# Two transformer layers with experts on one core: neighbours' steps at other places in the expert loops, unread matmuls in TensorE's waits, weight remainders in VectorE's waits

## The chip, the cores and the metric

The kernel runs on one NeuronCore of a Trainium2 chip. The metric is the device time of one launch in microseconds (us). Five engines take part: TensorE (PE in the rows, PEld for its weight loads), VectorE (DVE), ScalarE (ACT), GpSimd (POOL) and SyncE (SP), which issues all DMAs. Each engine runs its own list of instructions in order and waits on semaphores for the others.

## What is computed

Four sequences of 1024 tokens, 128 wide, go through two layers. Each is attention, add, layer norm, mixture of experts, add, layer norm:

```python
x = L0_attn_x                                        # (4, 1024, 128)
x = _layernorm(x + _L0_attn_ref(x, Wqkv, Wout))      # causal, 16 heads of 8, scores clipped
x = _layernorm(x + _L0_ffn_ref(x, Wg, W1, W2, W3))   # 8 experts, silu(x W1) * (x W2), W3, best 2
x = _layernorm(x + _L1_attn_ref(x, w_qkv, w_out, b)) # full attention, rotary, 16 heads
x = _layernorm(x + _L1_ffn_ref(x, rW1, ..., be2))    # 4 experts, gelu, best 2, router with a hidden layer
```

## The kernel before

There are five stages: the projections of the first layer, causal attention (to 300 us), the **first experts** (to 681 us), full attention (to some 1366 us) and the **last experts**. Every expert runs on all tokens; the gates make the choice.

**Expert stages.** The tokens are cut into eight chunks of 512. A chunk is 16 steps (`SPC`), a step is one slice of 128 hidden units. All products are made in three parts, from the upper halves and the remainders ("lo") of both factors. In step n of the first experts TensorE issues, in this order, what stands *beside* the step (`pe_beside`), the six matmuls of the hidden slice n+3 (`pe_hidden`, L1031) and the three of the product of slice n (`pe_product`, L1134). In the last experts the hidden slice has three matmuls and leads by five steps. VectorE does in its step n the multiply of slice n (L1447), the remainder of slice n-1 (L1436), what stands beside step n-2 (n-4 in the last experts, `LATE`), and in every second step the weighing of one expert's output by its gate (`dve_weigh`, L1427). ScalarE does silu (L1240) and the upper half (L1233) of a slice, and then what stands beside step n-2.

**Beside.** While chunk c runs, the chunk ahead ("front", c+1) is prepared and the chunk behind ("back", c-1) is finished. The steps of `plan` say at which n each piece stands: `o_proj` output projection, residual and statistics; `norm` the normalise of the front (L1292, tile xs); `x_turn` its transposes on TensorE (L946) and the two copies on ScalarE (L1209, L1210); `router` the gate scores (L1102) and the best two (from L1300); `weigh` gate weights; `g_turn` gates transposed; `y_turn` the transposes of the back's sum y_sb (L1053), residual and statistics (L1354); `norm2` its normalise (x_out) and a copy on ScalarE (L1190); `x2_turn`, `q`, `k`, `v` the next layer's projections (L1066, L1072). In the last experts `hidden` and `router` are the router's two layers (L1094, L1108). ScalarE's list has the copy of x_out ahead of the copies of `x_turn` where both stand beside the same step. `x2_turn` also waits for the front's best two (semaphore gate_pre), since it overwrites the bank with the gate scores.

**Ahead of the first experts** the front of chunk 0 is made with nothing running beside it. There VectorE also makes the remainders w_lo of the two hidden weights (L1486, after the normalise) and of the third weight, w3_lo (L1490, printed as w_lo too), after everything else.

**Behind the first experts** the back of chunk 7 is made with nothing beside it, apart from the first maxima of full attention: a "pair" is two score matmuls (L689) and one VectorE maximum over 1024 columns (L808), through a ring of two banks. Eight pairs stand beside the back (`BESIDE_BACK`), twenty more follow in `pe_full`, then the scores and the rounds of attention begin (16 rounds; in each, ScalarE makes 64 exponentials of 512 columns, L771).

## Time and profile before

| | us |
|---|---|
| median of 3 runs | 1602.66 (1599.79 to 1603.99) |
| the profiled execution | 1611.3 |
| its span in the trace | 1609.5 |
| TensorE busy | 1471.5 (91%) |
| VectorE busy | 1400.4 (87%) |
| ScalarE busy | 1202.9 (75%) |
| GpSimd busy | 307.5 (19%) |

No engine is idle long, and which one sets the pace changes from stage to stage. The page is therefore read by stage: the granted clock of TensorE first (full speed is 2.4 GHz, half is 1.2 GHz), then TensorE's idle times and what ended each.

### The profile page before, as it was taken

How to read it: one execution, taken by the hardware profiler on the slowest of the kernel's cores; microseconds unless marked ns; L12 is line 12 of the kernel's file. 1: busy time of each engine (PE TensorE's matmuls, PEld its weight loads, DVE VectorE, ACT ScalarE, POOL GpSimd, SP SyncE). 2: the span in 40 equal slices, each digit the busy share in tenths (PEclk: the TensorE clock that was granted, in tenths of full speed). 3: DMA queues.
4: the chain of work that ended last, by engine and by line, in shares of the span. 5: the costliest groups of instructions: out<-in, count | busy, mean ns of one | idle time of the engine just before them, and what ended most of it. 6: DMA issues, size and time to landing. Idle time of an engine off the chain costs nothing.

```text
span 1609.5 us, 32282 instructions
## 1 busy us (share of the span) xinstructions
PE 1471.5 (91%) x11200; PEld 797.1 (50%) x11200; DVE 1400.4 (87%) x2394; ACT 1202.9 (75%) x1897; POOL 307.5 (19%) x325
## 2 busy tenths in 40 slices
PE   7989898689999999969999999999999998999996
PEld 4333333377777777623333333333333334777775
DVE  5899999878888988887999999999999973788886
ACT  4999999644445454417999999999999986777775
POOL 0000000234455454420000000000000001234333
PEclk9899999799999998966999999999999997999999
DMA  6636432131224431111111111111111110211211
GB/s 203 203 106 182 120 102 86 49 107 40 96 93 127 128 108 66 66 41 51 46 37 37 46 45 38 42 37 36 37 36 36 37 32 28 69 56 63 75 56 40
DMA packets 71026, 116.76 MB, mean 73 GB/s; under 512 B 23808, under 2 KB 33920, under 8 KB 70272
## 3 DMA queue, kind: packets, MB, share of 16 engines
q1 hardware_dynamic: 70912, 115.21, 23.5%
q8 instruction: 75, 1.23, 0.3%
q14 instruction: 39, 0.32, 0.1%
HBM read 73.49 MB, written 41.16 MB: 71 GB/s over the span
## 4 chain that ended last, share of the span: by engine, by line
PE 61%; DVE 15%; ACT 10%; issue 10%; POOL 1%; DMA 1%; DVEq 0%; ACTq 0%; SPq 0%; POOLq 0%
PE full_o L718 14%; PE hid_pair L1031 12%; PE max_pair L689 11%; ACT cprobs L491 7%; PE bank L1134 7%; DVE negmax_h L808 5%; PE score L703 4%; PE causal_o L463 3%; PE triple L447 2%; PE bank L1066 2%; ACT o_sb L779 1%; DVE st L1284 1%; PE hid_pair L952 1%; PE bank L1094 1%; DVE hid_lo L1458 1%
## 5 line engine op out<-in xcount | busy, mean ns | idle before, releaser
L771 ACT ACTIVATE probs<-score 128x512 f32<-128x512 f32 x1024 | 546.6, 596 | 89.5 <-PE score L703 69.5
L808 DVE TENSOR_REDUCE negmax_h<-max_pair 128x2 f32<-128x1024 f32 x512 | 588.6, 1216 | 24.9 <-PE max_pair L689 24.8
L718 PE MATMUL full_o<-probs,v_st 128*32 128x256 f32 x4096 | 337.9, 403 | 17.7 <-ACT o_sb L779 17.7
L703 PE MATMUL score<-q_st,k_st 32*128 32x512 f32 x1024 | 319.9, 510 | 2.6 <-ACT probs L771 2.6
L689 PE MATMUL max_pair<-k_st,q_st 32*128 32x512 f32 x1024 | 264.7, 515 | 12.2 <-DVE negmax_h L808 10.8
L491 ACT ACTIVATE cprobs<-triple 128x1536 f32<-128x1536 f32 x192 | 258.4, 1713 | 5.2 <-PE triple L447 5.2
L689 PEld LDWEIGHTS max_pair<-k_st,q_st 32*128 32x128 f32 x1024 | 97.8, 188 | 236.7 <-DVE negmax_h L808 179.9
L1240 ACT ACTIVATE act_s<-hid_pair 128x512 f32<-128x512 f32 x128 | 76.7, 599 | 149.5 <-PE hid_pair L1031 149.5
L1031 PE MATMUL hid_pair<-x_hi,w_hi 128*128 128x512 f32 x384 | 171.3, 446 | 1.8 <-DVE x_lo L1401 1.0
L521 DVE TENSOR_SCALAR cprobs<-cprobs 128x1536 f32<-128x1536 f32 (+6 forms) x272 | 160.7, 618 | 2.9 <-ACT cprobs L491 2.9
L463 PE MATMUL causal_o<-cprobs,v_st 128*32 128x512 f32 (+3 forms) x1536 | 156.2, 502 | 2.2 <-DVE cprobs L521 2.2
L718 PEld LDWEIGHTS full_o<-probs,v_st 128*32 128x32 f32 x4096 | 83.3, 109 | 150.0 <-issue 94.5
L703 PEld LDWEIGHTS score<-q_st,k_st 32*128 32x128 f32 x1024 | 141.6, 187 | 28.8 <-ACT probs L771 19.5
L1031 PE MATMUL hid_pair<-x_lo,w_hi 128*128 128x512 f32 x384 | 154.6, 403 | 0.0
L1031 PE MATMUL hid_pair<-x_hi,w_lo 128*128 128x512 f32 x384 | 154.3, 402 | 0.0
L447 PE MATMUL triple<-q_st,k_st 32*128 32x512 f32 (+3 forms) x768 | 101.5, 429 | 28.7 <-ACT cprobs L491 26.0
L447 PEld LDWEIGHTS triple<-q_st,k_st 32*128 32x128 f32 x768 | 47.6, 186 | 135.5 <-ACT cprobs L491 127.1
L1248 ACT ACTIVATE hid_hi<-hid_pair,be 128x512 fp32r<-128x512 f32 x128 | 89.0, 695 | 24.9 <-PE hid_pair L1031 17.9
L1134 PE MATMUL bank<-hid_hi,w_hi 128*128 128x512 f32 x256 | 101.9, 398 | 1.4 <-DVE qk_lo L1436 1.3
L1134 PE MATMUL bank<-hid_hi,w_lo 128*128 128x512 f32 x256 | 101.4, 396 | 0.0
L568 POOL COPY v_st<-v_all 128x256 f32<-128x256 f32 x32 | 12.7, 400 | 434.6 <-PE causal_o L463 246.3
L520 DVE SCALAR_TENSOR_TENSOR cprobs<-cprobs,bound 128x256 f32<-128x256 f32 (+4 forms) x160 | 92.3, 577 | 3.9 <-ACT cprobs L491 2.5
(157 smaller groups left out, 2001.8 us busy)
## 6 DMA issues: line engine op xcount, KB each, us to landing
gate_all<-gate_scr SPq DMA_DIRECT2D x48, 512.0 KB, 4.3
o_scr<-o_sb SPq DMA_DIRECT2D x64, 256.0 KB, 2.1
k_st<-k_scr SPq DMA_DIRECT2D x64, 128.0 KB, 2.8
q_st<-q_scr SPq DMA_DIRECT2D x128, 64.0 KB, 2.5
k_st<-k_scr SPq DMA_DIRECT2D x64, 96.0 KB
q_st<-q_scr SPq DMA_DIRECT2D x64, 96.0 KB
q_scr<-qk_hi SPq DMA_DIRECT2D x18, 256.0 KB, 4.6
k_scr<-qk_hi SPq DMA_DIRECT2D x18, 256.0 KB, 4.5
```

The lines of the kernel that those rows point to most:

```text
L447: last = nc.tensor.matmul(triple[n % 2][:, bk, off:off + w], k_st[p][rows, kt * P:(kt + 1) * P], q_st[p][rows, q0:q0 + w], start=True, sto ...
L463: last = nc.tensor.matmul(causal_o[qc][SLOT * j:SLOT * (j + 1), c0:c0 + w], v_st[p][:, kt, j, :], cprobs[at % CP][:, bk, off:off + w], sta ...
L491: nc.scalar.activation(cprobs[n % CP][:, :, :], triple[n % 2][:, :, :], ACT.Exp, scale=SCALE).then_inc(L.exp_done, 1)
L520: nc.vector.scalar_tensor_tensor(edge, edge, float(np.exp(-CLIP)), limit, ALU.max, ALU.min)
L521: ins = nc.vector.tensor_scalar(plain, plain, float(np.exp(-CLIP)), float(np.exp(CLIP)), ALU.max, ALU.min)
L689: last = nc.tensor.matmul(ring[slot][:, k, :], q_st[p][rows, qt * P:(qt + 1) * P], k_st[p][rows, half * CH:(half + 1) * CH], start=True, s ...
L703: nc.tensor.matmul(sbank[L.score_bank(e)][:, :], k_st[p][rows, kt * P:(kt + 1) * P], q_st[p][rows, q0:q0 + w], start=True, stop=True, tile ...
L718: last = nc.tensor.matmul(full_o[SLOT * j:SLOT * (j + 1), cols], v_st[p][:, kt, j, :], probs[s % NP][:, j, cols], start=(kt == 0 and part ...
L771: nc.scalar.activation(probs[s % NP][:, L.HEADS[j], :], sbank[L.score_bank(e)][:, :], ACT.Exp, scale=SCALE).then_inc(L.exp_done, 1)
L808: nc.vector.tensor_reduce(negmax_h[:, qt // TPC, half, heads[0]:heads[1] + 1:2, qt % TPC], ring[slot][:, :, :], AXX, ALU.max, negate=True) ...
L1031: last = nc.tensor.matmul(hbank[2 * k + n % h_banks[layer]], w[:, slice_of(n)], x[:, :], start=(a == 0), stop=(a == 2))
L1134: last = nc.tensor.matmul(y_bank[e % 2], w, x, start=(f == 0 and a == 0), stop=(f == per - 1 and a == 2))
```

## The change

1. **Steps of the first experts' plan** are spread: y_turn 2 to 3, norm2 4 to 6, x2_turn 6 to 8, q 7 to 9, k 8 to 11, v 9 to 12, norm 3 to 4, x_turn 4 to 6, router 5 to 7, weigh 8 to 10, g_turn 10 to 13. The pairs beside the last back follow them. GpSimd's order gets the additions of y_sb (`pool_add`) moved between its other work.
2. **Steps of the last experts' plan** from x_turn on come one step later (x_turn, hidden, router, weigh); the gates are transposed in step 2 of their chunk (`GATES_AT`).
3. **Unread matmuls** (`pe_keep_busy`: ident times the rope table, fp32, 512 columns or half of it, into a bank that nobody reads then): one before the front of chunk 0, three after its step 1, one after its step 6; two and two in steps 2 and 3 of the last back; one of 256 columns after each of the twenty pairs.
4. **Remainders**: w_lo of the first weight goes before VectorE's wait for the output projection, that of the second behind the statistics, w3_lo behind the normalise and before x_lo.

```diff
-    BESIDE_BACK = {1: (0,), 2: (1,), 4: (2, 3), 7: (4,), 8: (5, 6), 9: (7,)}
+    BESIDE_BACK = {2: (0,), 3: (1,), 6: (2, 3), 9: (4,), 11: (5, 6), 12: (7,)}
...
             for m in first_pairs(L):
                 pe_pair(pe, L, 0, 0, m, m, m % 2)
+                pe_keep_busy(bank[0], 1, CH // 2)
...
-        for pl, steps in ((plan[0], (2, 4, 6, 7, 8, 9, 1, 1, 3, 4, None, 5, 8, 10)),
-                          (plan[1], (5, 7, None, None, None, None, 1, 1, 3, 6, 8, 11, 13, None))):
+        for pl, steps in ((plan[0], (3, 6, 8, 9, 11, 12, 1, 1, 4, 6, None, 7, 10, 13)),
+                          (plan[1], (5, 7, None, None, None, None, 1, 1, 3, 7, 9, 12, 14, None))):
...
-        GATES_AT, WEIGH_AT = 1, 1
+        GATES_AT, WEIGH_AT = 2, 1
...
+        BUSY_FRONT, BUSY_BACK = {1: 3, 6: 1}, {2: 2, 3: 2}
...
+        def pe_keep_busy(to, many, cols):
+
+            for _ in range(many):
+                nc.tensor.matmul(to[:, 0:cols], ident[:, :], rope_a[:, 0:cols], start=True, stop=True)
...
             if layer == 0:
+                pe.wait_ge(rope_loaded, 16 * 2)
+                pe_keep_busy(hbank[0], 1, CH)
                 for n in range(SPC):
                     pe_beside(pe, st, n, None, 0, 0, layer)
+                    if n in BUSY_FRONT:
+                        pe_keep_busy(hbank[0], BUSY_FRONT[n], CH)
...
                     pe_pair_beside_back(pe, layers[1], n)
+                    if n in BUSY_BACK:
+                        pe.wait_ge(st.v_saved, 2 * B - 1)
+                        pe_keep_busy(bank[2], BUSY_BACK[n], CH)
...
-                if n == (plan[0].norm, plan[1].x_turn)[layer]:
-
-                    for k in range(2):
+                if layer == 0 and n == plan[0].norm:
+                    dve.wait_ge(st.w3_upper, 1)
+                    nc.vector.tensor_tensor(w3_lo[:, :, :], w3[:, :, :], w3_hi[:, :, :].bitcast(F32),
+                                            ALU.subtract).then_inc(st.w3_lower, 1)
+                for k in ((0,) if n == plan[0].o_turn - 1 else (1,) if n == plan[0].o_proj else ()) if layer == 0 else (
+                        (0, 1) if n == plan[1].x_turn else ()):
```

**VectorE ahead of the first experts**, from the division (ot) on, before:

```order
L1377 TENSOR_TENSOR ot<-o_raw,o_rcp 128x512
L553 RECIPROCAL s_rcp<-s_raw 128x64
L1384 TENSOR_TENSOR res<-x_tm,bank 128x512
L1284 BN_STATS st<-res 128x6 x4
L1287 BN_AGGR mv<-st 128x2 x4
L1292 TENSOR_SCALAR xs<-res,mv,rstd 128x128 x4
L1486 TENSOR_TENSOR w_lo<-w_raw,w_hi 128x2048 x2
L1401 TENSOR_TENSOR x_lo<-xt,x_hi 128x512
```

The same stretch after, with the changed kernel's line numbers:

```order
L553 RECIPROCAL s_rcp<-s_raw 128x64
L1503 TENSOR_TENSOR w_lo<-w_raw,w_hi 128x2048
L1398 TENSOR_TENSOR res<-x_tm,bank 128x512
L1298 BN_STATS st<-res 128x6 x4
L1301 BN_AGGR mv<-st 128x2 x4
L1503 TENSOR_TENSOR w_lo<-w_raw,w_hi 128x2048
L1306 TENSOR_SCALAR xs<-res,mv,rstd 128x128 x4
L1498 TENSOR_TENSOR w_lo<-w,w_hi 128x2048
L1415 TENSOR_TENSOR x_lo<-xt,x_hi 128x512
```

The second w_lo now stands between the statistics (mv), which release GpSimd's rstd, and the normalise (xs), which waits for it.

**VectorE in the second chunk of the first experts**, steps 4 to 6, before (the multiply of slice 4 first):

```order
L1447 TENSOR_TENSOR o_sb<-hid_pair,act_s 128x512
L1436 TENSOR_TENSOR qk_lo<-hid,hid_hi 128x512
L1354 TENSOR_TENSOR res<-xs,bank 128x512
L1284 BN_STATS st<-res 128x6 x4
L1287 BN_AGGR mv<-st 128x2 x4
L1427 TENSOR_TENSOR y_sb<-bank,gate_all 128x512
L1447 TENSOR_TENSOR hid<-hid_pair,act_s 128x512
L1436 TENSOR_TENSOR qk_hi<-o_sb,hid_hi 128x512
L1292 TENSOR_SCALAR xs<-res,mv,rstd 128x128 x4
...
L1292 TENSOR_SCALAR x_out<-res,mv,rstd 128x128 x4
```

After, steps 4 to 8, up to the same x_out:

```order
L1461 TENSOR_TENSOR o_sb<-hid_pair,act_s 128x512
L1450 TENSOR_TENSOR qk_lo<-hid,hid_hi 128x512
L1441 TENSOR_TENSOR y_sb<-bank,gate_all 128x512
L1461 TENSOR_TENSOR hid<-hid_pair,act_s 128x512
L1450 TENSOR_TENSOR qk_hi<-o_sb,hid_hi 128x512
L1368 TENSOR_TENSOR res<-xs,bank 128x512
...
L1306 TENSOR_SCALAR xs<-res,mv,rstd 128x128 x4
L1441 TENSOR_TENSOR o_sb<-bank,gate_all 128x512
...
L1306 TENSOR_SCALAR x_out<-res,mv,rstd 128x128 x4
```

The weighing into y_sb now stands before the statistics of the back, so it is behind TensorE's transposes of y_sb, which are a step later; between xs and x_out there are two steps more and one weighing.

**TensorE at the start of full attention**, before and after:

```order
L1072 MATMUL bank<-w_qkv,xt 128x128 x4
L689 MATMUL max_pair<-k_st,q_st 128x512 x42
L703 MATMUL score<-q_st,k_st 128x512 x8
```

```order
L1074 MATMUL bank<-w_qkv,xt 128x128 x4
L689 MATMUL max_pair<-k_st,q_st 128x512 x4
L1155 MATMUL bank<-rope_a,ident 128x256
L689 MATMUL max_pair<-k_st,q_st 128x512 x2
```

Of the 21 pairs in one row before, the first is the last one beside the back; each of the twenty others has an unread matmul of 256 columns behind it now (the last two rows go on in turn).

## Rows read from the trace of the kernel before

**Rows 1.** Page, part 2: granted clock in tenths, 40 equal slices of the span.

```profile
PEclk9899999799999998966999999999999997999999
```

**Rows 2.** Windows: stretch, length, busy us of PE, PEld, DVE, ACT, POOL; clock, DMA.

```profile
397.50:444.20 46.70, 43.06 (x194) 33.65 (x193) 40.63 (x93) 22.38 (x41) 22.93 (x19) 0.96 0.28 92
608.00:619.00 11.00, 10.90 (x36) 8.63 (x37) 7.49 (x27) 4.00 (x8) 3.97 (x3) 0.56 0.00 0
684.00:694.00 10.00, 5.82 (x17) 2.86 (x18) 6.42 (x16) 1.23 (x2) 3.18 (x6) 0.52 0.00 0
...
706.00:725.00 19.00, 13.27 (x37) 4.78 (x35) 18.97 (x20) 0.00 (x0) 0.42 (x2) 0.50 0.22 68
725.00:757.00 32.00, 31.26 (x203) 10.41 (x201) 20.62 (x20) 21.10 (x40) 0.42 (x2) 0.51 0.01 2
...
1436.10:1466.40 30.30, 28.28 (x136) 22.43 (x136) 25.13 (x73) 22.67 (x37) 11.97 (x9) 1.00 0.20 64
```

**Rows 3.** Timeline, TensorE, first experts: start, us, line, [idle before <- who ended it].

```profile
336.03 0.99 PE L946 MATMUL bank<-ident,xs 128*128 128x128 f32 x4 [4.81 <-DVE xs L1292]
422.38 0.66 PE L946 MATMUL bank<-ident,xs 128*128 128x128 f32 x4 [2.43 <-DVE xs L1292]
426.34 1.03 PE L1102 MATMUL bank<-wg,xt 128*128 128x8 f32 x8 [1.21 <-ACT x_hi L1210]
```

**Rows 4.** Timeline of the same chunk, VectorE and ScalarE.

```profile
412.37 0.69 DVE L1447 TENSOR_TENSOR hid<-hid_pair,act_s 128x512 f32<-128x512 f32 x1
423.45 1.11 DVE L1292 TENSOR_SCALAR x_out<-res,mv,rstd 128x128 f32<-128x128 f32 x4
424.59 0.63 ACT L1190 ACTIVATE x_tm<-x_out 128x512 f32<-128x512 f32 x1 [3.22 <-DVE x_out L1292]
```

**Rows 5.** VectorE's multiplies two light steps apart; one step of TensorE in the chain.

```profile
402.07 0.69 DVE L1447 TENSOR_TENSOR o_sb<-hid_pair,act_s 128x512 f32<-128x512 f32 x1
...
406.26 0.69 DVE L1447 TENSOR_TENSOR o_sb<-hid_pair,act_s 128x512 f32<-128x512 f32 x1
...
402.09 1.37 PE hid_pair L1031 x6
403.46 0.69 PE bank L1134 x3
```

**Rows 6.** Timeline ahead of the first experts: VectorE's remainders, GpSimd beside them.

```profile
307.40 1.04 POOL L1519 TENSOR_TENSOR rstd<-rstd,mhalf 128x4 f32<-128x4 f32 x1
309.51 4.49 DVE L1486 TENSOR_TENSOR w_lo<-w_raw,w_hi 128x2048 fp32r<-128x2048 f32 x2
...
316.52 2.99 POOL L1542 TENSOR_TENSOR p<-euler,lead 128x4 f32<-128x4 f32 x1 [8.07 <-DVE lead L1303]
```

**Rows 7.** Timeline behind the first experts: fp32 matmuls, pairs, maxima.

```profile
696.53 1.96 PE L1066 MATMUL bank<-xt,w_qkv 128*128 128x512 f32 x4 [1.04 <-DVE rot L1371]
703.26 0.50 PE L689 MATMUL max_pair<-k_st,q_st 32*128 32x512 f32 x2 [0.63 <-DVE negmax_h L808]
713.64 12.50 DVE L808 TENSOR_REDUCE negmax_h<-max_pair 128x2 f32<-128x1024 f32 x11
722.80 0.79 PE L689 MATMUL max_pair<-k_st,q_st 32*128 32x512 f32 x2 [0.34 <-DVE negmax_h L808]
```

**Rows 8.** Timeline: first exponentials; first values after each save of an output.

```profile
725.24 5.13 ACT L771 ACTIVATE probs<-score 128x512 f32<-128x512 f32 x10 [21.42 <-PE score L703]
...
757.95 0.64 PE L718 MATMUL full_o<-probs,v_st 128*32 128x256 f32 x8 [0.58 <-ACT o_sb L779]
776.94 0.64 PE L718 MATMUL full_o<-probs,v_st 128*32 128x256 f32 x8 [0.57 <-ACT o_sb L779]
```

**Rows 9.** Timeline, TensorE, one chunk of the last experts.

```profile
1436.14 0.66 PE L946 MATMUL bank<-ident,xs 128*128 128x128 f32 x4 [1.12 <-DVE xs L1292]
1440.12 1.95 PE L1094 MATMUL bank<-xt,rw 128*128 128x512 f32 x4 [0.56 <-DVE mv L1287]
1457.41 0.60 PE L1118 MATMUL bank<-ident,gts 128*8 128x128 f32 x4 [0.33 <-DVE gts L1344]
```

More of the change, by code:

```diff
@@ L1488, in dve_end @@
             if layer == 0:
-                dve.wait_ge(st.w3_upper, 1)
-                nc.vector.tensor_tensor(w3_lo[:, :, :], w3[:, :, :], w3_hi[:, :, :].bitcast(F32),
-                                        ALU.subtract).then_inc(st.w3_lower, 1)
                 dve.wait_ge(rope_loaded, 16 * 2)
@@ L1581, in pool_experts0 @@
                     pool_rstd(pool, pc, st.stats2, st.rstd2, 1, c)
+                if c < 2 * B:
+                    pool_add(pool, st, c, 1, 0)
                 if front:
@@ L1584, in pool_experts0 @@
                 if c < 2 * B:
-                    pool_add(pool, st, c, 1, 0)
+                    pool_add(pool, st, c, 2, 0)
                 if front:
@@ L1588, in pool_experts0 @@
                 if c < 2 * B:
-                    pool_add(pool, st, c, 2, 0)
+                    pool_add(pool, st, c, 3, 0)
                 if c > 0:
-                    for a in range(2):
-                        pool_rot(pool, st, c - 1, a)
+                    pool_rot(pool, st, c - 1, 0)
                 if c < 2 * B:
-                    pool_add(pool, st, c, 3, 0)
+                    pool_add(pool, st, c, 4, 0)
+                if c > 0:
+                    pool_rot(pool, st, c - 1, 1)
+                if c < 2 * B:
+                    pool_add(pool, st, c, 5, 0)
                 if c > 0:
@@ L1597, in pool_experts0 @@
                         pool_qk_lower(pool, st, c - 1, a)
-                if c < 2 * B:
-                    pool_add(pool, st, c, 4, 0)
-                    pool_add(pool, st, c, 5, 0)
         def pool_experts1(pool, st):
```

## Prediction

> **What bounds the kernel now.** I read the granted clock first [rows 1, 2]. TensorE runs at 2.4 GHz in nearly all slices; two consecutive slices near 700 us show six tenths. The windows say where: from 684 to 694 us, and from 706 to 757 us, it is at 1.2 GHz (0.50 to 0.52 of full speed). Then I read TensorE's idle times in the stages that the change touches and what ended each [rows 3, 7, 9], and last the lists of the engines that ended them [rows 4 to 6, 8].
>
> Full attention is ScalarE's at full clock: one half round takes 776.94 - 757.95 = 18.99 us [rows 8], of which 32 exponentials and a save fill nearly all. At 1.2 GHz it is TensorE's: from 725 to 757 us it is busy 31.3 of 32.0 us and ScalarE only 21.1 [rows 2]. The expert stages are TensorE's, with waits. One step of the first experts takes 1.37 + 0.69 = 2.06 us of TensorE [rows 5]; a chunk with all that stands beside it is about 16 x 2.06 + 8 = 41 us (the 8 are my estimate from the fp32 row [rows 7]: q and k are 1.96 us each, o_proj and v half of it, and five groups of transposes and gate scores a quarter). It takes 46.7 [rows 2]. The missing 5.7 are a wait of 2.43 for xs, one of 1.21 for x_hi [rows 3], and some 2 us for a stretch of about 4 us at half clock behind them (clock 0.96 over the window [rows 2]: (1 - 0.96) x 46.7 = 1.9). There are six such chunks, and the first, with a wait of 4.81 [rows 3]. A chunk of the last experts takes 30.3 us, of which TensorE is busy 28.3 at full clock [rows 2]; its waits of 1.12, 0.56 and 0.33 us [rows 9] are exactly the rest.
>
> **Part by part.** The sums are made in the trace (span 1609.5, execution 1611.3 us). Its execution is 8.6 us above the median; nothing in the rows ties that to a stage, so I take the differences off the median unchanged.
>
> *Start of full attention: -9.* Each of twenty pairs costs VectorE 12.50 / 11 = 1.14 us, and that is the pace [rows 7]. At full clock a pair is 0.50 us of TensorE with 0.63 idle. The unread matmul has half the columns of one fp32 matmul of 512; two of those took 1.96 us [rows 7], so it is about 0.45. It fits into 0.63: nothing is lost, and TensorE's busy share rises from 44% to 84%. The clock was at 1.00 just there, around 703 us (0.50 us per pair), and was gone by 706. With 84% I expect it to stay, as it stays in the stretches where TensorE is busy more than nine tenths. The attention then starts at full clock: the first save comes behind 40 exponentials, at (18.99 - 0.6) / 32 = 0.575 us each, 23.0 us after 725.24, so the next values at about 748.9, not 757.95 [rows 8]. That is -9.0. Bounds: 0 if the clock falls anyway, -9.5. I take -9, nearest to the row of the half round at full clock.
>
> The clock: the Trainium skill ("TensorE: Matmul & The Clock Gate", Part 1) says that the half rate is the default and that activity releases it. The trace agrees in that the clock fell where pairs left TensorE idle. It does not agree that work alone brings it back at once: 725 to 757 us was 98% busy at 0.51. By the page's rule the sum stays as it is.
>
> *Last back: -1.* Two and two unread matmuls (0.9 us each at full clock) go into idle times of 2.6 and 2.6 us before the transposes of y_sb and the third pair; the row is the window, busy 5.8 of 10 us at 0.52 [rows 2]. If the clock holds, the q projection, on the path, takes half, -1.7; the wait for x_out before it is not filled, and can let the clock fall again. 0 to -2.5; I take -1.
>
> *Ahead of the first experts: -0.5.* Taken out of the path: the two w_lo, 4.49 us [rows 6], between the normalise and x_lo, of which some 2 us were exposed (TensorE needs x_hi and the gate scores in that time anyway). Put in: the second w_lo, 4.49 / 2 = 2.25 us, starts when the statistics end, at the moment at which GpSimd wants to make rstd. The row for such a meeting: GpSimd's power, 1.04 us alone, took 2.99 us beside w3_lo [rows 6], which VectorE issues just before it. So rstd would come about 2 us later, and xs with it. -2 + 2, and 0.5 for w3_lo gone from the end. The unread matmuls there lie in waits of VectorE's chain; at half clock the one after x_turn takes 1.8 us and can delay the gate scores by up to 1. Range -3 to +2.
>
> The Trainium skill ("SBUF — State Buffer", Who interferes with whom) says that a VectorE instruction with two inputs in SBUF and a GpSimd one that reads SBUF exclude each other for a whole instruction. That is what this row shows, and it is a rule against this edit: without it the sum here would be -2.5.
>
> *First chunk: -3.* The 4.81 us are VectorE standing at the weighing of step 4 until the gates' DMA lands. Now x_turn is at 6, not 4; TensorE gets through one more hidden slice (1.37) and is released before the normalise instead of after it (1.1). That is -2.5, and -0.5 for the clock behind it. Range -1 to -4.5.
>
> *Six chunks of the first experts: 0.* Spreading the steps looks like a gain here; by the rows it is hardly one. The gate scores wait for x_hi, x_hi stands in ScalarE's list behind the copy of x_out, which waited 3.22 us for VectorE's norm2 [rows 4]. norm2 and x_turn stood at the same step (4 and 4), and they do again (6 and 6). VectorE's way from the multiply of step 3 (412.37) to the end of norm2 (424.56) was 12.2 us. After the change the same pieces are on it, and two light steps with one weighing more: 4.19 us by the multiplies two light steps apart; their five instructions at 0.69 us [rows 5], a little overlapped, make 3.1 to 3.5, and I put the rest down to GpSimd's additions and to waits. TensorE gains two steps, 4.12 us. So the gate scores come 0 to 1.0 us better. Against that, the weighing into y_sb now stands behind TensorE's transposes at step 3 (0.4 us by when TensorE gets there), and the reciprocal (0.54 us) is now ahead of the best two, for which x2_turn waits. The wait for xs nearly goes (2.43 to about 0.4), that for x_hi grows (1.21 to about 3), and the clock falls as before. Per chunk -1 to +1, six chunks: -6 to +6; and the stretch of 11 us at 0.56 behind one of them [rows 2], which cost 5 instead of 2, may or may not come back: -3. I take 0, with -9 to +6.
>
> *Last experts: -8.5.* x_turn, hidden and router come a step later, norm and y_turn do not. A step is 3 + 3 matmuls, 2.06 x 6 / 9 = 1.38 us [rows 5]. So TensorE asks for xs 1.38 us later (1.12 was the wait) and for the statistics 1.38 later (0.56, plus the 1.12 no longer lost before it). The loop through VectorE's chain and back through the router shortens by one step, 1.38, down to 28.9; TensorE's own work is 28.3. I take 1.2 for each of seven chunks. The gates come one step later too, and VectorE's first weighing of the chunk waits for their DMA; no wait of that kind stands in this stage's list of waits, but a slack of under 1.4 us would turn the step into one. Bounds: 0 (that, or VectorE's chain as the pace) to 7 x 2.0 = -14.
>
> Sum: -9 - 1 - 0.5 - 3 + 0 - 8.5 = **-22**, 1602.7 - 22 = **1580.7 us**.
>
> **Rivals.**
>
> *A. The spread does what its name says* in the six chunks: waits and low clock go, each 5.7 us shorter by the most, and by perhaps 3.5 with VectorE busy 40.6 us of a chunk. For it: the two heavy stretches of VectorE are farther apart, and the wait for xs goes in my own count. Against it: ScalarE's list. 6 x 3.5 = 21 more: 1560.
>
> *B. The clock falls in spite of the unread matmuls* before full attention. A pair is then 0.79 us and the unread matmul 0.9: 1.69 against 1.14, so TensorE sets the pace: 20 x 0.55 = 11, and the -9 don't come, unless the fuller array raises it after some pairs. With half of that: 1580.7 + 9 + 5 = 1595; with all of it 1601.
>
> *C. Slower.* In the first experts the one wait of about 3 us for x_hi is longer than any now, and is followed by the wait of x2_turn. If behind it the clock stays low as from 608 to 619 us (cost 5 instead of 2 us [rows 2]) in all seven chunks, and the waits grow by 0.8: 7 x 3.8 = 27, so 1580.7 + 27 = 1607. It decides from 3.2 us per chunk. Against it: in the chunk of 46.7 us the clock came back within some 4 us [rows 2].
>
> *D. The last experts gain nothing*, since VectorE's chain (weights, spread, residual, statistics) is one piece: 1580.7 + 8.5 = 1589.
>
> **How the numbers follow.** Forecast 0.45, A 0.2, B 0.12, C 0.05, D 0.13, and 0.05 for two rivals together or something not seen. The range is 1558 to 1598: it leaves out C, the worst of B and the best of A. What a measurement of this kernel can tell is 0.3%, 4.8 us. Faster by more (under 1597.9): forecast, A, D and most of B, 0.87. Within: the rest of B, 0.07. Slower (over 1607.5): C and what was not seen, 0.06.
>
> **What would show it.** Right: clock 1.00 from 702 to 757 us and the first half round 19 us after the lead-in; unread matmuls idle-free at 0.45 us; in the first experts no xs wait but one of 2.5 to 3.5 us before L1104 released by x_hi, chunks still 45 to 47 us; GpSimd's rstd near 309 us taking over 2 us; chunks of the last experts at 29.0 us. Wrong: chunks of 42 to 43 us in the first experts (A), pairs 1.7 us apart (B), clock low for over a third of a chunk (C), 30.3 again (D).

## The result, and the profile after

The changed kernel takes 1628.3 us in the median (1627.4 to 1632.7, four runs), the kernel before 1603.3 (1599.8 to 1606.6): a ratio of 1.0154, with a 95% interval of 1.0128 to 1.018. The change makes the kernel 25 us slower. 1580.7 was predicted, and the range ended at 1598. All times and ratios here are of fast runs; one slow execution of e9 (2075 us, granted clock 0.55) is left out of its ratio.

I split both spans at the same five marks: VectorE's multiply into ot (start of the first experts), the last copy of v on ScalarE (their end), the first exponential of full attention, the second save of its output (a round of attention has two), the last save (start of the last experts), the last x_out. Each time is the start of that instruction.

| stage, us | before | after | difference |
|---|---|---|---|
| to ot | 301.3 | 300.9 | -0.5 |
| first experts, to the last copy of v | 400.4 | 411.1 | +10.7 |
| pairs, to the first exponential | 23.5 | 38.5 | +15.0 |
| first round, to the second save | 51.0 | 52.7 | +1.7 |
| rest of full attention | 581.6 | 582.4 | +0.8 |
| last experts, to the last x_out | 248.0 | 241.6 | -6.4 |

So the loss stands in two places that the prediction had as -9 and as -4.5 (ahead of the first experts, first chunk, middle chunks and last back together), and the gain in the last experts is there.

Windows of the changed kernel (columns as in [rows 2]): one middle chunk of the first experts; the stretch ahead of the pairs; the pairs; the first round at low and at full clock; one chunk of the last experts.

```profile
415.70:463.70 48.00, 43.76 (x193) 33.42 (x192) 40.06 (x92) 22.43 (x41) 23.06 (x18) 0.96 0.28 93
...
706.00:712.00 6.00, 4.02 (x20) 2.02 (x18) 4.99 (x7) 1.22 (x3) 3.15 (x3) 1.00 0.01 3
712.00:750.00 38.00, 37.65 (x83) 15.89 (x83) 26.14 (x24) 2.01 (x4) 2.93 (x6) 0.51 0.14 42
750.00:787.00 37.00, 36.18 (x232) 11.66 (x233) 22.61 (x21) 24.25 (x46) 0.42 (x2) 0.50 0.10 25
787.00:806.00 19.00, 18.43 (x192) 7.27 (x184) 18.22 (x18) 17.33 (x33) 0.81 (x3) 0.98 0.42 139
1437.00:1466.20 29.20, 28.06 (x136) 21.89 (x135) 25.23 (x70) 22.13 (x37) 11.95 (x9) 1.00 0.22 67
```

From 712 to 787 us the clock is at 1.2 GHz, though TensorE is busy 73.8 of 75 us. In the kernel before, it was low from some 705 to 756 us [rows 2]. TensorE's timeline at the first unread products (L1155), start and duration first:

```profile
712.35 0.50 PE L689 MATMUL max_pair<-k_st,q_st 32*128 32x512 f32 x2 [0.64 <-DVE negmax_h L809]
712.78 1.22 PE L1155 MATMUL bank<-rope_a,ident 128*128 128x256 f32 x2
713.94 0.79 PE L689 MATMUL max_pair<-k_st,q_st 32*128 32x512 f32 x2
714.66 1.22 PE L1155 MATMUL bank<-rope_a,ident 128*128 128x256 f32 x2
715.81 0.79 PE L689 MATMUL max_pair<-k_st,q_st 32*128 32x512 f32 x2
```

The last pair at full clock (0.50) is the one ahead of the first unread product. From then on a pair and its product take 715.81 - 713.94 = 1.87 us, against the 1.14 us of VectorE's maxima [rows 7]. 0.73 us more, twenty times, is 14.6 of the 15 us.

In the first experts, TensorE's longest wait, and ScalarE's list ahead of its end (two timelines, one chunk):

```profile
386.40 1.03 PE L1104 MATMUL bank<-wg,xt 128*128 128x8 f32 x8 [3.04 <-ACT x_hi L1224]
```

```profile
384.66 0.63 ACT L1204 ACTIVATE x_tm<-x_out 128x512 f32<-128x512 f32 x1 [3.09 <-DVE x_out L1306]
385.19 0.58 ACT L1223 ACTIVATE xt<-bank 128x512 f32<-128x512 f32 x1
385.67 0.59 ACT L1224 ACTIVATE x_hi<-bank 128x512 fp32r<-128x512 f32 x1
```

This wait stands in six chunks, 3.04 us each time, where [rows 3] had 2.43 for xs and 1.21 for x_hi. The xs wait is gone. (In the kernel before, the wait of 1.21 stands in two of the six chunks only, at 426 and 519 us; in the other four it is 0.1 us or less.) From the first o_proj in the stage's rows to the eighth, one chunk after another: ot to the second o_proj 22.2 us, now 23.2; the next distance 42.8, now 43.8; the five behind it 231.2 (46.2 each), now 239.3 (47.9 each); the rest to the last copy of v 104.2, now 104.8. So 8.1 of the 10.7 us lie in the five distances, 1.6 each. The sixth chunk with such a wait lies in the rest.

### The profile page after: what moved, and what is told of

Same layout as the page of the kernel before. It is cut to its first block, busy times and chain, and to the rows that moved or that the text cites. A ratio compares the mean times of both kernels' runs of the same rounds, so it can differ in the third digit from the quotient of the medians.

```text
span 1630.9 us, 32398 instructions
## 1 busy us (share of the span) xinstructions
PE 1505.0 (92%) x11258; PEld 806.1 (49%) x11258; DVE 1401.9 (86%) x2394; ACT 1202.5 (74%) x1897; POOL 307.0 (19%) x325
## 4 chain that ended last, share of the span: by engine, by line
PE 56%; DVE 18%; issue 12%; ACT 10%; POOL 2%; DMA 1%; DVEq 0%; ACTq 0%; SPq 0%; POOLq 0%
PE full_o L718 14%; PE max_pair L689 11%; PE hid_pair L1033 9%; ACT cprobs L491 7%; PE bank L1136 5%; DVE negmax_h L809 4%; PE score L703 4%; PE causal_o L463 3%; PE triple L447 2%; PE bank L1155 1%; DVE qk_lo L1450 1%; DVE st L1298 1%; DVE qk_hi L1450 1%; PE bank L1068 1%; ACT o_sb L780 1%
## 5 line engine op out<-in xcount | busy, mean ns | idle before, releaser
L568 POOL COPY v_st<-v_all 128x256 f32<-128x256 f32 x32 | 12.6, 399 | 434.2 <-PE causal_o L463 245.3
```

## The experiments

Ratios are to the kernel before on the same chip, with their 95% interval. After them stand, from each profile, the stages that tell the kernels apart:

| kernel | ratio (95%) | first experts | pairs | first round | last experts |
|---|---|---|---|---|---|
| before | 1 | 400.4 | 23.5 | 51.0 | 248.0 |
| changed | 1.0154 (1.0128 to 1.018) | 411.1 | 38.5 | 52.7 | 241.6 |
| e11, changed again | 1.0153 (1.0127 to 1.018) | 408.0 | 38.5 | 48.6 | 242.1 |
| e1 | 1.003 (1.0012 to 1.0047) | 410.0 | 23.5 | 44.3 | 242.8 |
| e7 | 1.0018 (0.9998 to 1.0037) | 413.2 | 23.5 | 44.5 | 242.2 |
| e14 | 1.0077 (1.005 to 1.0103) | 398.1 | 38.8 | 48.4 | 249.5 |
| e2 | 0.9959 (0.9942 to 0.9976) | 398.0 | 23.5 | 47.7 | 240.6 |
| e3 | 1.0063 (1.0036 to 1.0089) | 409.0 | 23.5 | 51.7 | 247.5 |
| e4 | 1.0005 (0.9985 to 1.0024) | 399.8 | 23.5 | 47.7 | 248.7 |
| e5 | 1.0072 (1.0046 to 1.0097) | 415.6 | 23.5 | 44.3 | 242.4 |
| e9 | 0.9982 (0.9965 to 0.9999) | 401.6 | 23.5 | 44.4 | 243.2 |
| e6 | 0.9946 (0.9925 to 0.9967) | 394.2 | 23.5 | 44.5 | 242.3 |
| e8 | 0.9963 (0.9943 to 0.9982) | 397.3 | 25.9 | 44.8 | 243.6 |
| e10 | 0.9947 (0.9926 to 0.9968) | 397.6 | 23.5 | 46.7 | 241.8 |
| e12 | 0.9999 (0.998 to 1.0017) | 407.3 | 23.5 | 44.2 | 241.7 |
| e13 | 0.9912 (0.9892 to 0.9932) | 393.6 | 23.5 | 47.9 | 242.3 |

One profile is one execution. Where the first experts are those of the kernel before they take 398.0, 398.1 and 399.8 us (e2, e14, e4) beside its 400.4, and the changed kernel has 411.1 and 408.0 (e11). So a difference of some 3 us between two profiles shows nothing in this stage.

**The products behind the pairs: e1, e7, e14, e11, e8.** e1 is the changed kernel without

```
             for m in first_pairs(L):
                 pe_pair(pe, L, 0, 0, m, m, m % 2)
-                pe_keep_busy(bank[0], 1, CH // 2)
```

> The changed kernel without the one TensorE product of 256 columns behind each of the twenty pairs ahead of the full attention; everything else as changed. Theory (the products themselves are the loss: at half clock one takes 1.15 us beside a pair of 0.7 us, and VectorE's 12.5 us per chunk no longer sets the pace): pairs at 1.1 to 1.2 us each as before, from the last copy of v to the first exponential about 24 us instead of 38.5, and about 1613 us against 1628 of the changed kernel. Rival (the stretch is long because the last chunk's later steps put q, k and v into a low clock, products or not): the stretch stays above 32 us and the time above 1622. Second rival (the products are of use later, in the start of the full rounds): up to 6 us of the gain are given back there, 1617 to 1620.

The pairs take 23.5 us again, and of the 1.5% over the kernel before 0.3% is left. That is some 20 us by the ratios and 15 by the pairs; the intervals leave room for the difference. The theory holds, and the last rival was the wrong way round: the first round became 8 us shorter, not longer. Was that the work of the other unread products, beside the last chunk's late steps? e7 takes those away too (the three lines under `if n in BUSY_BACK`):

> The changed kernel without the products behind the pairs and without those beside the last chunk's late steps (the two and two of 512 columns); those ahead of the first chunk stay. Theory (the products beside the late steps hold the full clock longer, so the low clock begins later and is over 10 us behind the first exponential instead of 31 to 37): without them the clock falls by 702 us and comes back some 30 us behind the first exponential, 5 to 7 us more than the kernel with them (1611.7). Rival (where the clock comes back is not set by them): within 2 us of 1611.7.

In the times the rival was right: the ratio is that of e1 within the intervals, and the first round takes 44.5 us as e1's 44.3. In the trace the products do something. TensorE in the last back, in the changed kernel (first three rows) and in e7:

```profile
692.18 1.98 PE L1155 MATMUL bank<-rope_a,ident 128*128 128x512 f32 x4
694.96 0.66 PE L1055 MATMUL bank<-ident,y_sb 128*128 128x128 f32 x4 [0.80 <-POOL y_sb L1576]
706.75 1.96 PE L1068 MATMUL bank<-xt,w_qkv 128*128 128x512 f32 x4 [0.75 <-DVE rot L1385]
```

```profile
694.70 0.92 PE L1054 MATMUL bank<-ident,y_sb 128*128 128x128 f32 x4 [2.73 <-POOL y_sb L1572]
707.69 3.75 PE L1067 MATMUL bank<-xt,w_qkv 128*128 128x512 f32 x4 [0.75 <-DVE rot L1381]
```

With them the clock is low for 3.4 us of this stretch (702.5 to 705.9; also 3.4 in e1 and e11), without them for 17.0 (695.0 to 712.0), and in e3 below, without them too, for 10.2. From the last product of the experts to the last copy of v it is 20.5 us with them (20.8 in e1) and 23.5 in e7, 21.3 in e3. That is 1 to 3 us, and the intervals of 0.2% can't show it. e14 puts the line that e1 removed into the kernel before, alone (with the function it calls):

> The kernel before with one unread fp32 product of 256 columns behind each of the twenty pairs and nothing else of the change. Theory (they cost by themselves, the clock being low there in either kernel): from the last copy of v to the first exponential 38.5 us instead of 23.5, and 15 us more in all, 1.0093 of the kernel before. Rival (the clock holds if it has not fallen at the first pair): the stretch stays below 30 us and the time within 6 us.

Pairs 38.8 us: the products cost 15 us there by themselves, and the ratio of 1.0077 agrees with the expected 1.0093 within its interval. The clock was at 1.2 GHz from the pair ahead of the first product on (0.79 us), in the changed kernel from the pair behind it: the price is the same. e11 is the changed kernel, unaltered:

> The changed kernel once more, beside the kernels above. Theory (the low clock over the pairs goes with this kernel: 75 us from the first product behind a pair to 37 us behind the first exponential): low for over 60 us again, 1.2 to 1.8% above the kernel before. Rival (where it comes back differs from execution to execution): it comes back within 20 us of the first exponential, with the pairs and their products still at 1.87 us, some 5 us less in the profiled time.

The ratio comes back to 0.0001. The clock comes back at 772.6 us, 24 us behind the first exponential; in the first profile of the same kernel it was 37. So this point differs between executions of one kernel (11 to 37 us over all profiles here), and the 44 to 53 us of the first round can't be put down to an edit from one profile. The times show it too: two of e3's five runs took 1614.2 and 1614.7 us at a mean clock of 0.960, the other three 1621.3 to 1624.0 at 0.952 to 0.954. Last, a lighter product in its place, rounded operands (fp32r), in e8, which is e6 below with

```
                 pe_pair(pe, L, 0, 0, m, m, m % 2)
+                nc.tensor.matmul(bank[0][:, 0:CH // 2], w_hi[0][:, 0:P],
+                                 w_hi[0][:, 0:CH // 2], start=True, stop=True)
```

> As the kernel before with the last experts' steps and the later copy to x_tm, and with one light unread product behind each of the twenty pairs: operands rounded to fp32r, 128 rows, 256 columns, which takes a quarter of an fp32 product's time. Theory (the fp32 products cost 1.15 us each at half clock and so lost 15 us; a light one fits into the wait of 0.34 us behind each pair): the pairs stay at 1.14 us each, nothing is lost. Whether the clock holds is open: if full rows hold it, the first round is 6 us shorter and the time 5 to 7 us less than without them; if a clock once fallen stays low through this stretch whatever fills it, within 2 us.

Windows and timeline of e8, over the pairs and behind them:

```profile
702.00:723.60 21.60, 21.55 (x54) 9.79 (x54) 21.45 (x20) 0.00 (x0) 0.42 (x2) 0.50 0.19 62
723.60:735.00 11.40, 10.71 (x61) 4.17 (x61) 5.08 (x5) 8.39 (x16) 0.06 (x1) 0.50 0.01 1
```

```profile
710.42 0.79 PE L689 MATMUL max_pair<-k_st,q_st 32*128 32x512 f32 x2
711.14 0.58 PE L760 MATMUL bank<-w_hi 128*128 128x256 f32 x1
711.65 0.79 PE L689 MATMUL max_pair<-k_st,q_st 32*128 32x512 f32 x2
```

TensorE is busy 21.55 of 21.6 us and stays at half clock all the same. A pair with the light product takes 1.23 us, still more than VectorE's 1.14: the pairs take 25.9 us, not the 23.5 that the theory expected. So neither kind of unread product held the clock over the pairs or brought it back there. In e8, e11 and the changed kernel the clock fell at the first of them, behind some 7 us of late steps and pairs in which TensorE had idle time (busy 4.02 of 6 us from 706 to 712); in e14 it had fallen one pair earlier. No run has unread products in those 7 us as well, so whether the clock can be kept up over the pairs is open.

**The last experts: e2.** The kernel before with the changed steps of the last experts alone:

```
-                          (plan[1], (5, 7, None, None, None, None, 1, 1, 3, 6, 8, 11, 13, None))):
+                          (plan[1], (5, 7, None, None, None, None, 1, 1, 3, 7, 9, 12, 14, None))):
-        GATES_AT, WEIGH_AT = 1, 1
+        GATES_AT, WEIGH_AT = 2, 1
```

> The kernel before with the last experts' steps alone of the change (turn of x at step 7, hidden layer at 9, router at 12, weighing at 14, gates at 2). Theory (the stage accounting of the two traces: the last experts went from 248.0 to 241.6 us, alone on their steps): a period of 29.2 instead of 30.3 us, 6 to 8 us less in all, about 1596 us against 1603. Rival (the gain came with the other parts, for instance the remainders or a differing start of the stage): within 2 us of the kernel before.

0.41% faster, 6.6 us, and 240.6 us in the stage where the kernel before has 248.0: this part is the whole gain, alone. A chunk:

```profile
1420.40:1449.60 29.20, 28.08 (x137) 22.34 (x136) 25.05 (x73) 22.46 (x37) 12.02 (x9) 1.00 0.20 67
```

29.2 us with TensorE's own 28.1 hardly changed against [rows 2]. The rest is two waits, of the three in [rows 9]; TensorE in this chunk:

```profile
1428.15 0.66 PE L946 MATMUL bank<-ident,xs 128*128 128x128 f32 x4 [0.54 <-DVE xs L1292]
1432.13 1.96 PE L1094 MATMUL bank<-xt,rw 128*128 128x512 f32 x4 [0.58 <-DVE mv L1287]
```

The wait for xs has halved (1.12 before), that for the statistics is as it was (0.56 before), that for the gates is gone.

**Ahead of the first experts: e4.** The kernel before with the weights' remainders moved and the unread products ahead of the first chunk.

> The kernel before with the remainders of the weights moved ahead (the two w_lo before and beside the first norm, w3_lo with it) and the unread products ahead of the first chunk (one, and three and one in the steps' gaps); steps, pairs and last experts as before. Theory (rstd on GpSimd meets the moved w_lo and takes 2 us, the chain over the norm gives back what VectorE gains): within 1.5 us of the kernel before, first hidden product at about 315 us from the start of the span as before. Rival (full clock ahead of the first experts): 2 us or more less.

No difference, as in the changed kernel, whose first hidden product starts at 314.95 us and not at 314.85. GpSimd and VectorE of the changed kernel, there:

```profile
306.45 1.99 POOL L1532 TENSOR_SCALAR rstd<-mv 128x4 f32<-128x4 f32 x1 [7.51 <-DVE mv L1301]
```

```profile
306.10 2.26 DVE L1503 TENSOR_TENSOR w_lo<-w_raw,w_hi 128x2048 fp32r<-128x2048 f32 x1
309.60 1.11 DVE L1306 TENSOR_SCALAR xs<-res,mv,rstd 128x128 f32<-128x128 f32 x4 [1.25 <-POOL rstd L1533]
```

The first of the two small instructions of rstd ends with the remainder beside it, and xs starts at 309.60 instead of 308.48: what VectorE saves behind, it loses here. Counted from ot, xs comes 1.6 us later and the first hidden product 0.5 us later (14.1 instead of 13.5; it is 12.6 in e2, e3 and e14, which have the old order).

**The first experts: e3, e5, e9.** e3 is the kernel before with the spread (the first experts' steps, the pairs' places and GpSimd's order):

```
-        for pl, steps in ((plan[0], (2, 4, 6, 7, 8, 9, 1, 1, 3, 4, None, 5, 8, 10)),
+        for pl, steps in ((plan[0], (3, 6, 8, 9, 11, 12, 1, 1, 4, 6, None, 7, 10, 13)),
```

> The kernel before with the first experts' steps, the pairs' places and GpSimd's order alone of the change; no unread products, remainders where they were, last experts as before. Theory (the spread itself makes a chunk 47.9 instead of 46.4 us, since x_hi on ScalarE waits behind the copy that norm2 needs from VectorE, 3.0 us per chunk): about 10 us more, 1613 us, the wait of 3 us ahead of the first hidden product by x_hi in every middle chunk. Rival (the loss in the first experts comes from the moved remainders or from the unread products around the first and last chunk): within 3 us of the kernel before.

409.0 us against 400.4, and a ratio of 1.0063 (10 us): the spread, with GpSimd's order, by itself makes the loss of this stage, with the wait of 3.05 us in all six chunks. By the trace ScalarE's list looked like the cause. e5 takes the copy from the head of the list, in e1:

```
             if back is not None:
-                if layer == 0 and n == pl.norm2:
+                if layer == 0 and n == pl.norm2 + 1:
                     act.wait_ge(st.norm2, back + 1)
```

> The changed kernel without the products behind the pairs, and with ScalarE's copy of x_out to x_tm (first experts) one step later, behind the copies xt and x_hi instead of ahead of them. Theory (head of ScalarE's list: the copy waits 3.10 us for VectorE's x_out, and xt and x_hi, whose source has been ready for 3 us, wait behind it; TensorE then waits 3.04 us and runs some 4 us at half clock): the wait ahead of the router's product goes, the middle chunks take 43 to 45 us instead of 47.8, and the time is 16 to 24 us less than that of the same kernel without this edit, against 1611.7 some 1588 to 1596. Rival (VectorE with 40 us of work per chunk in its own order is the bound, and ScalarE's wait only shows it): another wait takes the place, the period stays above 47 us and the time within 4 us.

This theory fell. The wait for x_hi is gone and the kernel is slower by 0.4% in the median (the intervals just touch) and by 5.6 us in the stage. TensorE's transposes of x_out and VectorE's top-2 ahead of them, in e1 (first two fences), then in e5:

```profile
437.96 0.72 PE L946 MATMUL bank<-ident,x_out 128*128 128x128 f32 x4
```

```profile
437.46 0.17 DVE L1316 TENSOR_TENSOR lead<-mx 128x4 f32<-128x4 f32 x1
```

```profile
437.75 0.84 PE L946 MATMUL bank<-ident,x_out 128*128 128x128 f32 x4 [4.18 <-DVE lead L1316]
```

```profile
437.44 0.17 DVE L1316 TENSOR_TENSOR lead<-mx 128x4 f32<-128x4 f32 x1
```

Top-2 ends at the same moment, 437.6, with the copy here or there, and x2_turn at step 8 follows it at once. It writes the bank in which the router's product of step 7 lies, and may do so only when VectorE has read it. In e5 VectorE goes from 420.8 us to that point without a wait, with the statistics for norm2, both normalises, three weighings, the reciprocals and the top-2 in its list beside two instructions for each step; in e1 with one wait, of 1.56 us behind ScalarE's act_s. That e5 without this wait gets no further has its reason in two remainders beside which GpSimd works; VectorE in e1 (first two rows) and in e5:

```profile
429.98 0.68 DVE L1449 TENSOR_TENSOR qk_lo<-hid,hid_hi 128x512 fp32r<-128x512 f32 x1
434.45 0.77 DVE L1449 TENSOR_TENSOR qk_hi<-o_sb,hid_hi 128x512 fp32r<-128x512 f32 x1
```

```profile
430.15 1.53 DVE L1449 TENSOR_TENSOR qk_lo<-hid,hid_hi 128x512 fp32r<-128x512 f32 x1
433.83 1.38 DVE L1449 TENSOR_TENSOR qk_hi<-o_sb,hid_hi 128x512 fp32r<-128x512 f32 x1
```

They take 2.91 instead of 1.45 us: GpSimd's x_lo and its addition to y_sb run at 429.84 and 433.39 in e5 and at 433.39 and 434.63 in e1. So the copy's move gave VectorE 1.56 us and took 1.46 from it. The wait for x_hi only used up time that TensorE would have stood one step later. The low clock shows why e5 even loses: it lasts 3.4 us in both, but in e1 (434.8 to 438.2) it is nearly over when x2_turn starts, and in e5 (438.0 to 441.4) it lies over the products between x2_turn and q (2.6 us apart in e1, 4.1 in e5; q starts at 440.59 and 441.88). e9 gives VectorE one step more, in e5:

```
-        (3, 6, 8, 9, 11, 12, 1, 1, 4, 6, None, 7, 10, 13)
+        (3, 6, 9, 10, 11, 12, 1, 1, 4, 6, None, 7, 10, 13)
-    BESIDE_BACK = {2: (0,), 3: (1,), 6: (2, 3), 9: (4,), 11: (5, 6), 12: (7,)}
+    BESIDE_BACK = {2: (0,), 3: (1,), 6: (2, 3), 10: (4,), 11: (5, 6), 12: (7,)}
```

> As the changed kernel without the products behind the pairs and with the later copy to x_tm, and now with the turn of x2 at step 9 and q at 10 instead of 8 and 9 (k and v stay at 11 and 12), first experts. Theory (what the copy's move uncovered: the turn of x2 may only write its bank when VectorE's top-2 of the router's product has read it; the change put the reciprocals and the top-2 into the one step between the router's product at 7 and the turn at 8, at the end of 17 us in which VectorE has no wait; TensorE waits 4.0 us for it): with a step more the wait of 4 us falls to under 1.5, middle chunks of 45 to 47 us instead of 48.9, and 12 to 24 us less than the same kernel without this edit (1618.7), some 1595 to 1607. Rival (VectorE is the bound of the whole chunk, 41.5 of 49 us busy): the wait moves to q or k and the period stays above 48.

The theory held: 0.9% faster than e5, 401.6 us instead of 415.6. TensorE, and the window of one chunk:

```profile
434.52 0.63 PE L946 MATMUL bank<-ident,x_out 128*128 128x128 f32 x4 [1.37 <-DVE lead L1316]
446.59 1.16 PE L1073 MATMUL bank<-w_qkv,xt 128*128 128x128 f32 x8 [1.57 <-DVE rot L1384]
```

```profile
411.80:458.40 46.60, 42.49 (x193) 32.42 (x192) 42.84 (x92) 22.62 (x41) 22.66 (x18) 1.00 0.28 93
```

The wait fell from 4.2 to 1.4 us, the clock stays full. The change had kept that distance at one step and had put the reciprocals into it. But 46.5 us per chunk is no better than the kernel before, with 46.2.

**The same head of the list in the kernel before: e6.** e5's edit, in e2.

> The kernel before with the last experts' steps of the change, and with ScalarE's copy of x_out to x_tm one step later, behind xt and x_hi. Theory (same head of the list as in the changed kernel, but smaller: TensorE waits 1.21 us for x_hi there): the waits of 1.2 us go, 1 to 1.5 us per chunk in six or seven chunks, 6 to 10 us less than the same kernel without this edit (1599.8), about 1592. Rival (the 4.8 and 2.4 us waits for the hidden product's other input grow by what this one gives): within 3 us.

A ratio of 0.9946 beside e2's 0.9959: the intervals overlap, so a gain of 2 us is not shown by the times. In the profile the two waits of 1.21 are gone, in the same two chunks stand waits of 2.05 and 2.03 us for the top-2, and the chunks take 45.9 instead of 46.2 us in the mean. The rival has most of it: here, too, VectorE's list was behind ScalarE's.

**Another spread: e10, e12, e13.** With that knowledge a spread that keeps the early steps and puts two steps between router and x2_turn, in e6:

```
-        (2, 4, 6, 7, 8, 9, 1, 1, 3, 4, None, 5, 8, 10)
+        (2, 4, 8, 9, 10, 11, 1, 1, 3, 5, None, 6, 9, 11)
-    BESIDE_BACK = {1: (0,), 2: (1,), 4: (2, 3), 7: (4,), 8: (5, 6), 9: (7,)}
+    BESIDE_BACK = {1: (0,), 2: (1,), 4: (2, 3), 9: (4,), 10: (5, 6), 11: (7,)}
-                if layer == 0 and n == pl.norm2 + 1:
+                if layer == 0 and n == pl.norm2 + 2:
```

> The kernel before with the last experts' steps of the change and its first experts spread in another way: y_turn 2, norm 3 and norm2 4 stay, the turn of x moves from 4 to 5, the router from 5 to 6, the turn of x2 from 6 to 8, q, k, v from 7, 8, 9 to 9, 10, 11, weighing 8 to 9, gates 10 to 11, and the copy to x_tm behind xt and x_hi. Theory (the waits of 2.4 us for xs and of up to 2 us for the top-2 are one step too few each for VectorE's list; more steps behind them are enough): both go, middle chunks of 43 to 44.5 us instead of 45.9, 9 to 16 us less than with the old steps (1598.0), about 1585. Rival (VectorE busy 42.2 of 45.9 us is the bound): a period of 45 or more and less than 5 us gained.

The waits for xs and top-2 are gone and the period is still 45.9, as the rival said; instead TensorE has a wait of 1.5 us for one of VectorE's multiplies in each chunk. VectorE's timeline has where it went:

```profile
445.06 0.69 DVE L1427 TENSOR_TENSOR o_sb<-bank,gate_all 128x512 f32<-128x512 f32 x1 [2.73 <-POOL y_sb L1562]
```

It has no wait from 405 to 442 us and then waits for GpSimd, whose addition stands behind both sums of rot. e12 gives it the changed kernel's order of GpSimd's list (the last part of the diff).

> As the kernel with the half spread, and with the changed kernel's order of GpSimd's list (the additions of y_sb taken between the sums of rot, both subtractions for qk_lo last). In the half spread VectorE waits 2.73 us per chunk for GpSimd's addition to y_sb, which stands behind the second sum of rot in GpSimd's list. Theory (that wait took up what the spread gave): it goes, the middle chunks take 43.5 to 45 us instead of 45.9, and the time is 6 to 14 us less than with the half spread alone (1597.3). Rival (VectorE's own work, 41.9 us in a chunk of 45.9 us, beside TensorE's 43.1, is the bound, and other waits of VectorE or TensorE of the same size follow): a period above 45.3 us and less than 4 us gained.

Slower again by 0.5% (407.3 us): neither theory nor rival had a loss. VectorE's wait turned up elsewhere; ScalarE and VectorE of e12:

```profile
446.76 0.63 ACT L1199 ACTIVATE qk_hi<-rot 128x512 fp32r<-128x512 f32 x1 [3.56 <-POOL rot L1524]
```

```profile
448.86 0.69 DVE L1447 TENSOR_TENSOR o_sb<-hid_pair,act_s 128x512 f32<-128x512 f32 x1 [3.28 <-ACT act_s L1240]
```

In the mean of the middle chunks the period is 47.2 us. Now the second sum of rot stands behind an addition that itself waits 3.84 us for VectorE's weighing; ScalarE's qk_hi waits for the sum, the copies of v and gates and act_s behind it, and VectorE for act_s. e13 moves one addition only, in e10:

```
+                if c < 2 * B:
+                    pool_add(pool, st, c, 3, 0)
                 if c > 0:
                     for a in range(2):
                         pool_rot(pool, st, c - 1, a)
-                if c < 2 * B:
-                    pool_add(pool, st, c, 3, 0)
```

> As the kernel with the half spread, with one addition to y_sb moved in GpSimd's list, from behind both sums of rot to ahead of both; the rest of its order is that of the kernel before. Theory (the full reordering lost because the second sum of rot came behind an addition that waits for VectorE, and ScalarE's list with it; the wait of 2.73 us of VectorE in the half spread is an addition that came too late): VectorE's wait falls below 1 us, no wait of 3 us on ScalarE for rot comes, the middle chunks take 43.5 to 45.2 us instead of 45.9, 4 to 14 us less than the half spread (0.9947 of the kernel before), about 0.988 to 0.992 of it. Rival (any chunk of this kernel ends near 45.9, since VectorE's list of 42 us with what GpSimd's transfers add to it is the bound): a period of 45.5 or more, and 0.994 to 0.996.

0.9912, 14 us less than the kernel before, and the only version here that is clearly faster than e2. The chunk, and the one wait of VectorE that is left in it:

```profile
409.40:454.90 45.50, 42.63 (x193) 32.40 (x192) 42.48 (x93) 22.71 (x41) 21.95 (x18) 1.00 0.30 95
```

```profile
444.66 0.69 DVE L1447 TENSOR_TENSOR o_sb<-hid_pair,act_s 128x512 f32<-128x512 f32 x1 [1.81 <-ACT act_s L1240]
```

The 2.73 us are gone, no wait of 3 us is there, and the period fell only from 45.9 to 45.4 in the mean. The ratio is as the theory said, the period is between the two forecasts (45.2 and 45.5), and VectorE's wait of 1.81 is above the 1 us expected. VectorE is busy 42.5 of 45.5 us and TensorE 42.6; that one of them is the bound is not shown. By the profiles e13's first experts are 4 us shorter than e10's; the median says 0.35%, and the intervals still overlap. No run has the changed steps with the old order of GpSimd's list. In the half spread the new order costs 1.3 us per chunk (45.9 to 47.2), so a part of e3's loss may be its; the wait for x_hi is not, since e5 takes it away with that order in place.

## Why the prediction was wrong, step by step

*Start of full attention (-9 predicted, +15 measured, and +1.7 in the first round).* The step that failed is "with 84% I expect it to stay". The clock fell at the first product, and from then on TensorE's busy share was no guide: busy 37.65 of 38 us at 0.51. I had the row that speaks against it in my own text, 725 to 757 us at 98% busy and 0.51 [rows 2], and drew nothing from it for the sum. Rival B named the case, at 0.12, and its price was too low: 0.9 us for the product, my 0.45 at full clock doubled, where the trace has 1.15 from start to start (714.66 to 715.81), so 1.87 and not 1.69 per pair, 15 and not 11 us. e14 shows that price alone.

*Last back (-1).* From the last product of the experts to the last copy of v it was 21.1 us and is 20.5, so -0.6, by the clock as the prediction said: low for 3.4 us and not 10.2. e7, without these products, has 23.5. The longer distance from the last chunk's o_proj on (104.2 us, now 104.8) also holds most of the sixth middle chunk with its loss. The ratios of e1 and e7 can't resolve so little.

*Ahead of the first experts (-0.5).* Right that the two terms cancel: rstd meets the remainder (1.99 us), e4 is 1.0005. Each is smaller than said: xs comes 1.6 us later and not 2, and the first hidden product 0.5 us later and not 0.5 earlier, so some 1 us was taken out of the path and not 2.5. The rule of the Trainium skill ("SBUF — State Buffer", Who interferes with whom) stood for the +2, and the row agrees with it.

*First chunk (-3).* The stall went from 4.81 to 3.63 us and not to some 2.3. The stretch from ot over the first chunk grew by 2.0 us (22.2 + 42.8, now 23.2 + 43.8), but e11, the same kernel, has 20.2 + 42.2 and e2, with the old steps, 20.9 + 42.8. So neither the 3 us nor a loss is shown.

*Middle chunks (0, -9 to +6 predicted; +8.1 in the five distances).* The wait for xs went and that for x_hi came to 3.04 us (about 3 was said), with the low clock behind it. The step that failed is the sum per chunk, "the gate scores come 0 to 1.0 us better". From the start of o_proj to the gate scores it was 14.2 us in the mean and is 18.6: 4.4 more, with 4.1 of TensorE's two steps to set against it, so 0.3 worse. VectorE's way from the multiply of step 3 to the end of norm2 takes 16.7 us (415.87 to 432.56) and not 12.2 plus 3.1 to 4.1; 0.7 of it is the weighing that now waits for the transposes of y_sb, which the text named (0.4) and left out. VectorE and TensorE in this chunk of the changed kernel:

```profile
421.51 0.69 DVE L1441 TENSOR_TENSOR y_sb<-bank,gate_all 128x512 f32<-128x512 f32 x1 [0.70 <-PE bank L1055]
431.45 1.11 DVE L1306 TENSOR_SCALAR x_out<-res,mv,rstd 128x128 f32<-128x128 f32 x4
```

```profile
426.15 0.47 PE L1033 MATMUL hid_pair<-x_hi,w_hi 128*128 128x512 f32 x1 [0.61 <-DVE o_sb L1461]
451.92 1.16 PE L1074 MATMUL bank<-w_qkv,xt 128*128 128x128 f32 x8 [0.43 <-DVE rot L1385]
```

The sum also took the wait of 1.21 us as one of every chunk, and it stands in two of six. TensorE's idle time per chunk was 3.16 us (xs 2.40, x_hi 0.48 in the mean, x_out 0.31) and is 4.15: x_hi 3.04 and the two waits above, of which the sum had none. That is 1.0 of the 1.6 us. The other 0.6 is busy time of TensorE, 43.1 and now 43.7 us; its cause is open.

The wait of x2_turn for the top-2 is 0.1 us or nothing in the changed kernel. It is what stood behind the wait for x_hi: I wrote that the reciprocal was now ahead of the top-2 (0.54 us) and gave it no place in the sum; e5 uncovered the wait, 4.0 to 4.2 us, and e9 took most of it away. Both steps together, the copy's and x2_turn's, make e9 0.5% faster than e1. Rival A and C both took the waits of TensorE for the cause. C's place (the first experts) was right, its mechanism (clock low for longer in each chunk) not: the clock was 0.96 as before. The stretch of 11 us at 0.56, of which 3 us might come back, was not a matter of the steps: at the same place the clock is low for 10.2 us in the kernel before and for 3.4 in e2, e4 and e14, which have its steps.

*Last experts (-8.5 predicted, -6.4 measured; e2: -6.6).* Right, a little less in size: 29.2 us per chunk where 29.0 was said, since 0.54 of the 1.12 us for xs and the 0.56 for the statistics stayed.

The sum of the parts measured alone, 1.0077 (e14), 1.0063 (e3), 0.9959 (e2) and 1.0005 (e4), is +1.04%, against 1.54% for all together. With intervals of 0.2 to 0.3% each, the difference may be chance or the parts may add to each other; that is not settled. e7, with the spread and without the two groups of products, has 1.0018 where e3, e2 and e4 add up to 1.0027.

## What to carry over

Where one engine goes through its list without a gap, or with a gap that its next instructions would use up, the longest wait of another engine need not be the cause: in e5, taking it away brought the next one up at the same moment. Look for the engine that has no idle time between two points and count the steps there. Work that only fills an engine needs its price at the lower clock, and a row that shows this clock holding or coming back at that place under such work; and each reordering of a helper engine's list is to be read for what stands behind its first waiting instruction.

## What the runs showed of the chip

The clock stayed at 1.2 GHz for 75 us with TensorE busy 98% of the time (half of it pairs of 32 rows with fp32 products of 128 rows between them, half the first round of attention), and 21.6 us with fp32r products at 21.55 busy. Where it comes back differs between executions of the same kernel: 37 and 24 us behind the first exponential for the changed kernel. Beside the last back, four unread fp32 products of 512 columns in TensorE's idle times went with a low clock of 3.4 us, against 10.2 and 17.0 us in two kernels with the same steps and without them. An fp32 product of 256 columns between products with other weights took 1.15 us from its start to that of the next at half clock, an fp32r one 0.51 (711.14 to 711.65). A VectorE remainder of 128x512 took 0.68 and 0.77 us (e1), and 1.38 and 1.53 us where GpSimd worked on tiles of that size at the same time (e5). The Trainium skill ("TensorE: Matmul & The Clock Gate", Part 1) says that activity releases the clock; over the stretches of 75 and 21.6 us the rows do not agree that activity is enough, and no run here shows what decides the moment.
